# A graph convolution on one core: DVE kept free for the copies of x, strips 2 to 11 in two steps

## The chip, the cores and the metric

The kernel runs on one core of one Trainium2 chip. The metric is the device time of one execution in microseconds (us), as the median of several runs.

## The reference

```python
# x: (8192, 128), adj: (8192, 8192), w: (128, 128), all fp32
A = adj + jnp.eye(adj.shape[0], dtype=adj.dtype)
deg = jnp.sum(A, axis=1)
d_isqrt = jax.lax.rsqrt(deg)
A_hat = A * d_isqrt[:, None] * d_isqrt[None, :]
h = jnp.matmul(A_hat, x)
y = jax.nn.elu(jnp.matmul(h, w))
out = _layernorm(x + y, axis=-1)
```

The matrix adj has 256 MiB. A product with rows of x needs the row sums of adj for those rows first, since x is scaled by d_isqrt before it is multiplied.

## The kernel before

adj is cut into 16 x 16 tiles of 512 x 512 (1 MiB each). Tile (t, u) holds the rows of strip u and the columns of band t. Strip r is the 16 tiles (0..15, r); when all its row sums are known, x of band r can be scaled, and only then can any tile of column r be multiplied. PE multiplies a column's tiles two to four at a time (a "part", L1016, 64 matmuls of 128 to 512 columns, each of which stands as two records in the trace), so that 256 records belong to 4 tiles when each matmul is 256 wide. Parts of one job gather in one of two PSUM sets.

A tile (t, r) with t < r comes after x of band t is known: it is loaded once ("first"), summed by ACT (L916), turned by DVE (a transposition of 32 x 32 blocks, L1035), multiplied, and its product is added to hT by DVE (L1060, L1062). A tile (t, r) with t >= r has to be loaded for the row sums of strip r before x of band t exists. Some of these are kept in SBUF until then ("near": the table KEPT says how many diagonals back for each column, 56 in all); the others are only summed ("far", four staging slots) and loaded a second time at the end ("again", 80 tiles). SBUF has 23 slots of one tile; a load waits on the SP queue (L824 to L855) until the slot's tenant has been multiplied.

How x of a band comes to be ready, for each strip: ACT's last row sum of the strip; DVE adds the sums up (L1042, the row sum reduction); POOL takes the power -0.5 (L881), and scales x (L888); then 16 copies spread x over the four quadrants: pair (s, q) is the rows of quarter s for quadrant q. The pairs (0, q) are needed for the first matmuls of a part: (0, 0) and (0, 1) are copied by DVE (L1049), (0, 2) and (0, 3) by ACT (L924). POOL copies the other twelve (L899). POOL also adds the unit matrix to the diagonal tile (L874). For the strips in HALVED, 3 to 9, the whole chain is done in two steps, blocks 0 and 1 first and then blocks 2 and 3 ("half 0" and "half 1"): the strip's near loads come in two halves, and PE may multiply one or two parts by half 0 alone while half 1 is being made.

The order of all this is fixed before the kernel is built: the function plan() walks through a rough model of the engines and writes for each engine a list of operations, picking at each moment, among what is ready for an engine, the one of the lowest rank (x's copies, reductions and scalings 0, adds 1, transpositions 4 or 6). FEED is the number of tiles that should wait for PE before the plan turns from first tiles to the next strip's rows. Each engine then executes its list in order, with semaphores; the plan's times are not in the kernel, only its order.

Of the kernel before, what the change touches and what calls it, by code (L numbers as in the profile page):

```python
# [7 lines left out]
Q = 4  # L8
BAND = 512
BANDS = N // BAND  # L10
BLOCKS = BAND // 128
# [1 line left out]
SLOTS = 23  # L13
STAGE = 4
LATE = 3
KEPT = (1, 2, 3, 4, 5, 6, 5, 4, 5, 4, 3, 4, 3, 2, 3, 2)
AHEAD = 2
STAY = 10
WIDTHS = (4, 2)
XN = 1  # L20
HALVED = range(3, 10)
HALF_JOBS = 2
PIECES = 2
RING = 4
SETS = 2
MERGE = 4
FEED = 10
FLIGHT = 4
EPS = 1e-5
LAST = 2  # L30
FIRST_COPIES = [("dve", [(0, 0), (0, 1)]), ("act", [(0, 2), (0, 3)]), ("pool", [(s, q) for s in (1, 2, 3) for q in range(Q)])]
LATE_COPIES = [("act", [(s, q) for q in range(Q)]) for s in range(Q)]


# [40 lines left out]
def plan():  # L75
# [28 lines left out]
    firsts, queued, rest, backlog = [], [], [], 0  # L104
    held_diagonals = {}
    group_at, group_todo, group_open, group_job = -1, [], [], None
    pending_x = []

    def offer(engine, rank, kind, arg, took):
        nonlocal serial  # L110
# [13 lines left out]
    def allowed(kind, arg):  # L124
        if kind == "out":
            return free_set() is not None and counts["residuals"] > 0 and counts["w"] > 0 and (counts["outs"] == counts["z"] or not parts_left())
        if kind == "z":
            return counts["stored"] >= arg - RING + 1
        return True

    def parts_left():
# [2 lines left out]
    def release(slot):  # L134

        if rows_done and len(late) < LATE:
            tenants[slot].append(("late", len(late)))
            late.append(slot)
            if len(late) == LATE:
                offer("act", 0, "residuals", 0, 0.6)  # L140
        else:
            free.append((now, slot))
# [183 lines left out]
    def close_stage():  # L326

        nonlocal stage_open
        if stage_open and rows_done and not far_open:
            stage_open = False  # L330
            for slot in range(STAGE):
                tenants[slot].append(("stage", 0))
                release(slot)

    def row_summed(load):

# [219 lines left out]
    while True:  # L556
        issue()
        for e in ready:
            if until[e] <= now:
# [9 lines left out]
                elif e == "pe" and (arg := next_part()) is not None:  # L569
                    kind, long = "part", took(len(parts[arg][2])) * (1.0 if parts[arg][5] is None else 1 / PIECES) + (1.75 if now - until["pe"] > 2.5 else 0.0)  # L570
                    lone_before = len(parts[arg][2]) == 1
                else:
                    continue
                order[e].append((kind, arg))
                until[e] = now + long
                busy[e] += long
# [554 lines left out]
```

## Time and profile before

| | |
|---|---|
| median of 3 runs | 1052.9 us (1051.27 to 1054.26) |
| the profiled execution | 1054.86 us, of which the span is 1053.1 us |
| PE busy | 924.1 us (88%) |
| DVE busy | 772.1 us (73%) |
| ACT busy | 702.9 us (67%) |
| POOL busy | 213.1 us (20%) |
| bytes moved by DMA | 368.37 MB, mean 350 GB/s |
| mean granted clock of PE | 0.968 |

The span is the time from the first to the last instruction; the execution's own time is 1.8 us longer. Busy shares are means over stages with different limits: in the first 680 us the DMA engines are full, in the rest PE is.

### The profile page before, as it was taken

What the parts mean: (1) busy time and instruction counts of PE and PEld (TensorE: products, weight loads), DVE (VectorE), ACT (ScalarE), POOL (GpSimd) and SP (SyncE); (2) the same over time, 40 slices, a digit from 0 to 9 for tenths busy, and PEclk for the clock granted to TensorE, in tenths of its full rate; (3) what the DMA queues carried; (4) which work ended last, traced back from release to release, by engine and by line L of the source; (5) the groups of instructions that cost most, each with busy time, mean ns of one, the idle gap of its engine ahead of it and who ended that gap; (6) DMA issues with size and microseconds to landing.
All of it is one profiled execution on the core that took longest, in us unless ns stands there. A gap on an engine that the chain in (4) does not pass through costs nothing.

```text
span 1053.1 us, 36270 instructions
## 1 busy us (share of the span) xinstructions
PE 924.1 (88%) x16256; PEld 858.6 (82%) x16256; DVE 772.1 (73%) x649; ACT 702.9 (67%) x1667; POOL 213.1 (20%) x365
## 2 busy tenths in 40 slices
PE   0089399399797998999999999999999999999995
PEld 0066288399797997999899999899889999999994
DVE  0496497576776768686879787887999698866923
ACT  6898798889988898988888988862132518131201
POOL 0120120210502204050522533457011001000000
PEclk9999789799998998999999999999999999999998
DMA  9999999999999999999999999977999888999920
GB/s 384 401 394 407 399 393 400 396 395 395 384 399 356 377 392 397 388 396 396 394 397 395 384 392 392 338 247 262 386 385 341 292 280 293 307 298 315 348 76 21
DMA packets 168092, 368.37 MB, mean 350 GB/s; under 512 B 6528, under 2 KB 33280, under 8 KB 159232
## 3 DMA queue, kind: packets, MB, share of 16 engines
q1 hardware_dynamic: 150896, 357.59, 91.1%
q10 hardware_dynamic: 17040, 8.46, 2.7%
q8 instruction: 128, 2.10, 0.8%
q14 instruction: 28, 0.23, 0.1%
HBM read 361.82 MB, written 4.19 MB: 348 GB/s over the span
## 4 chain that ended last, share of the span: by engine, by line
PE 66%; DMA 11%; POOL 7%; DVE 6%; issue 6%; ACT 3%; SPq 1%; POOLq 0%; ACTq 0%; DVEq 0%
PE p_set L1016 65%; DMA space<-in_adj 8%; POOL space L899 5%; DVE space L1035 4%; DMA xn<-in_x 3%; ACT space L916 1%; PE p_set L994 1%; ACT space L924 1%; POOL xn L888 1%; SPq L855 1%; DVE hT L1060 1%; POOL d L881 1%; POOL space L874 0%; DVE space L1049 0%; DVE stats L1096 0%
## 5 line engine op out<-in xcount | busy, mean ns | idle before, releaser
L1016 PE MATMUL p_set<-space 32*128 32x256 f32 (+2 forms) x16128 | 907.6, 383 | 115.8 <-DVE space L1035 55.4
L1016 PEld LDWEIGHTS p_set<-space 32*128 32x128 f32 x16128 | 843.2, 188 | 176.0 <-issue 121.2
L1035 DVE STREAM_TRANSPOSE space<-space 128x2048 f32<-128x2048 f32 x256 | 580.2, 2293 | 96.8 <-ACT space L916 69.9
L916 ACT ACTIVATE space<-space 128x512 f32<-128x512 f32 (+3 forms) x732 | 576.8, 790 | 80.7 <-DMA space<-in_adj 76.1
L1060 DVE TENSOR_TENSOR hT<-p_set,hT 128x1024 f32<-128x1024 f32 (+1 forms) x104 | 106.8, 1040 | 125.0 <-PE p_set L1016 124.8
L899 POOL COPY space<-xn 32x256 f32<-32x256 f32 (+1 forms) x276 | 134.2, 486 | 18.1 <-POOL space L874 1.5
L916 ACT ACTIVATION_READ_ACCUMULATOR space<-space 128x1 f32 x732 | 137.5, 188 | 0.0
L881 POOL TENSOR_TENSOR d<-deg,minus_half 128x2 f32<-128x2 f32 (+1 forms) x23 | 19.0, 827 | 517.5 <-DVE deg L1042 517.2
L939 ACT ACTIVATE space<-space 128x512 f32<-128x512 f32 x16 | 10.1, 632 | 161.4 <-DVE space L1071 161.3
L924 ACT ACTIVATE space<-xn 32x512 f32<-32x512 f32 (+1 forms) x110 | 63.1, 573 | 76.8 <-POOL xn L888 73.3
L906 POOL TENSOR_TENSOR rstd<-var_eps,minus_half 128x4 f32<-128x4 f32 x16 | 16.9, 1056 | 231.7 <-DVE var_eps L1105 231.6
L947 ACT ACTIVATE space<-space,shift,rstd 128x128 f32<-128x128 f32 x60 | 24.7, 481 | 22.3 <-DVE shift L1111 22.3
L888 POOL TENSOR_TENSOR xn<-xn,d 128x256 f32<-128x256 f32 (+1 forms) x27 | 22.1, 820 | 67.1 <-DMA xn<-in_x 65.5
L1049 DVE COPY space<-xn 32x256 f32<-32x256 f32 (+1 forms) x46 | 26.5, 576 | 11.0 <-POOL xn L888 10.0
L994 PEld LDWEIGHTS p_set<-ident,hT 128*128 128x128 f32 x128 | 15.4, 191 | 6.7 <-issue 4.3
L874 POOL TENSOR_TENSOR space<-space,ident 128x512 f32<-128x512 f32 x16 | 20.4, 1276 | 0.7
L994 PE MATMUL p_set<-ident,hT 128*128 128x128 f32 x128 | 18.2, 287 | 1.7 <-DVE hT L1060 1.7
L1062 DVE COPY hT<-p_set 128x1024 f32<-128x1024 f32 (+2 forms) x6 | 9.5, 1580 | 13.9 <-PE p_set L1016 13.9
L1090 DVE SCALAR_TENSOR_TENSOR space<-space 128x512 f32<-128x512 f32 x16 | 10.6, 663 | 11.1 <-ACT space L941 10.9
L1096 DVE BATCH_NORM_STATS2 stats<-space 128x6 f32<-128x128 f32 x64 | 14.0, 282 | 0.5
L1042 DVE TENSOR_REDUCE deg<-sums 128x2 f32<-128x34 f32 (+1 forms) x23 | 4.1, 178 | 13.7 <-ACT space L916 13.7
L1071 DVE TENSOR_TENSOR space<-p_set,d 128x512 f32<-128x512 f32 x16 | 10.8, 673 | 2.9 <-PE p_set L994 2.8
(16 smaller groups left out, 38.2 us busy)
## 6 DMA issues: line engine op xcount, KB each, us to landing
space<-in_adj SPq DMA_DIRECT2D x309, 1024.0 KB, 13.5
space<-in_adj SPq DMA_DIRECT2D x30, 512.0 KB, 10.7
space<-in_adj SPq DMA_DIRECT2D x16, 768.0 KB, 13.9
xn<-in_x SPq DMA_DIRECT2D x20, 256.0 KB, 11.4
space<-in_x ACTq DMA_DIRECT2D x16, 256.0 KB, 7.4
out_rows<-space ACTq DMA_DIRECT2D x16, 256.0 KB, 9.3
ident<-in_w ACTq DMA_DIRECT2D x1, 64.0 KB, 6.2
```

The costliest lines, as they stand in the source:

```text
L874: nc.gpsimd.tensor_tensor(on_diagonal, on_diagonal, ident[:, :].unsqueeze(1).to_broadcast([128, BLOCKS, 128]), ALU.add)\
L881: nc.gpsimd.tensor_tensor(d[:, r, blocks], deg[:, r % 2, blocks], minus_half[:, blocks], ALU.pow).then_inc(d_ready, 1)
L888: nc.gpsimd.tensor_tensor(xn[:, h % XN, blocks], xn[:, h % XN, blocks], d[:, t, blocks].unsqueeze(2).to_broadcast([128, many, F]), ALU.mul ...
L899: nc.gpsimd.tensor_copy(xs_part(h, half, q, s), x_part(h, half, s)).then_inc(copied_by["pool"], 1)
L916: ins = nc.scalar.activation(view[:, g], view[:, g], ACT.Copy, accum_out=to[:, g:g + 1])
L924: nc.scalar.activation(xs_part(h, half, q, s), x_part(h, half, s), ACT.Copy).then_inc(copied_by["act"], 1)
L947: ins = nc.scalar.activation(pos[:, n % RING, b], pos[:, n % RING, b], ACT.Identity, bias=shift[:, n % RING, b:b + 1], scale=rstd[:, n % R ...
L994: ins = nc.tensor.matmul(p[:, 0, F * b:F * (b + 1)], hT[:, at:at + 128], w_sb[:, :], start=True, stop=True)
L1016: ins = nc.tensor.matmul(to, xs_chunk(h, j)[quadrant(q)], moving, start=first and s == 0 and b == blocks_of(half).start, stop=last and s = ...
L1035: nc.vector.transpose(slots[slot], slots[slot]).then_inc(tile_turned, 1)
L1049: nc.vector.tensor_copy(xs_part(h, half, q, s), x_part(h, half, s)).then_inc(copied_by["dve"], 1)
L1060: nc.vector.tensor_tensor(rows, new, rows, ALU.add).then_inc(product_added, 1)
```

## The change

Four tables and one rule of the plan change.

- FIRST_COPIES: all four pairs (0, q) are DVE's; ACT copies none for the first use of a band.
- HOLD = 8: for strips 0 to 7, from the moment the plan gives ACT the last row sum of a strip (or of a half), DVE gets no transposition that would take 2.4 and no add that would take 1.3 beyond the end of that sum, until it has got the copies of that x.
- HALVED: strips 2, 10 and 11 are now also done in two steps.
- FEED 14 in place of 10.
- KEPT: column 15 keeps four tiles in place of two, so that (15, 12) and (15, 13) are loaded once. Loads of adj go from 336 to 334 MiB.

```diff
--- before.py
+++ after.py
@@ -13,22 +13,23 @@
 SLOTS = 23
 STAGE = 4
 LATE = 3
-KEPT = (1, 2, 3, 4, 5, 6, 5, 4, 5, 4, 3, 4, 3, 2, 3, 2)
+KEPT = (1, 2, 3, 4, 5, 6, 5, 4, 5, 4, 3, 4, 3, 2, 3, 4)
 AHEAD = 2
 STAY = 10
 WIDTHS = (4, 2)
 XN = 1
-HALVED = range(3, 10)
+HALVED = range(2, 12)
 HALF_JOBS = 2
 PIECES = 2
 RING = 4
 SETS = 2
 MERGE = 4
-FEED = 10
+FEED = 14
 FLIGHT = 4
+HOLD = 8
 EPS = 1e-5
 LAST = 2
-FIRST_COPIES = [("dve", [(0, 0), (0, 1)]), ("act", [(0, 2), (0, 3)]), ("pool", [(s, q) for s in (1, 2, 3) for q in range(Q)])]
+FIRST_COPIES = [("dve", [(0, q) for q in range(Q)]), ("pool", [(s, q) for s in (1, 2, 3) for q in range(Q)])]
 LATE_COPIES = [("act", [(s, q) for q in range(Q)]) for s in range(Q)]
@@ -126,6 +127,8 @@
             return free_set() is not None and counts["residuals"] > 0 and counts["w"] > 0 and (counts["outs"] == counts["z"] or not parts_left())
         if kind == "z":
             return counts["stored"] >= arg - RING + 1
+        if kind in ("turn", "add") and urgent:
+            return now + (2.4 if kind == "turn" else 1.3) <= min(urgent.values())
         return True
@@ -331,6 +334,19 @@
+    def last_sum(load):
+
+        r = load[3] if load[0] == "tile" else load[1]
+        k0, nk = (0, BLOCKS) if load[0] == "tile" else load[2:4]
+        wide = 1 if load[0] == "tile" else load[5] if load[0] == "near" else load[5] // BAND
+        for half in halves_of(r):
+            many = BLOCKS if half is None else BLOCKS // PIECES
+            base = many * half if half is not None else 0
+            rows = len(set(range(k0, k0 + nk)) & set(range(base, base + many)))
+            if rows and sums_left[r, half] == rows * wide:
+                return r, half
+        return None
@@ -571,6 +587,10 @@
                     lone_before = len(parts[arg][2]) == 1
                 else:
                     continue
+                if kind == "sum" and (row := last_sum(loads[arg])) is not None and row[0] < HOLD:
+                    urgent[row] = now + long + 0.1
+                elif kind == "copies" and e == "dve" and (homes[arg[0]][0], arg[1]) in urgent:
+                    del urgent[homes[arg[0]][0], arg[1]]
                 order[e].append((kind, arg))
                 until[e] = now + long
                 busy[e] += long
```

What this does to the order of DVE, at strip 7. TENSOR_REDUCE is the row sum reduction of a half, COPY from xn are the copies of x, STREAM_TRANSPOSE a tile's transposition, TENSOR_TENSOR on hT an add. Before:

```order
L1060 TENSOR_TENSOR hT<-p_set,hT 128x4x8x32 x2
L1042 TENSOR_REDUCE deg<-sums 128x2
L1049 COPY space<-xn 32x2x128 x2
L1035 STREAM_TRANSPOSE space<-space 128x4x512
L1042 TENSOR_REDUCE deg<-sums 128x2
L1060 TENSOR_TENSOR hT<-p_set,hT 128x4x8x32
L1035 STREAM_TRANSPOSE space<-space 128x4x512
L1049 COPY space<-xn 32x2x128 x2
L1035 STREAM_TRANSPOSE space<-space 128x4x512 x2
```

And now, at the same place:

```order
L1080 TENSOR_TENSOR hT<-p_set,hT 128x4x4x32 x2
L1062 TENSOR_REDUCE deg<-sums 128x2
L1069 COPY space<-xn 32x2x128 x4
L1062 TENSOR_REDUCE deg<-sums 128x2
L1069 COPY space<-xn 32x2x128 x4
L1080 TENSOR_TENSOR hT<-p_set,hT 128x4x8x32
L1055 STREAM_TRANSPOSE space<-space 128x4x512
L1080 TENSOR_TENSOR hT<-p_set,hT 128x4x8x32
L1055 STREAM_TRANSPOSE space<-space 128x4x512 x3
```

Two adds stood directly ahead of the first reduction, and two transpositions and one add between it and the second copies; now one job's add (in two pieces) stands ahead of it, and nothing but the four copies and the second reduction behind it, until both halves have been copied.

POOL at strips 10 and 11. The first TENSOR_TENSOR on d is the power, the one on xn the scaling, the one on space the unit matrix added to the diagonal tile, COPY the twelve copies of x. Before:

```order
L881 TENSOR_TENSOR d<-deg,minus_half 128x4
L888 TENSOR_TENSOR xn<-xn,d 128x512
L874 TENSOR_TENSOR space<-space,ident 128x4x128
L899 COPY space<-xn 32x4x128 x12
L881 TENSOR_TENSOR d<-deg,minus_half 128x4
L888 TENSOR_TENSOR xn<-xn,d 128x512
L874 TENSOR_TENSOR space<-space,ident 128x4x128
L899 COPY space<-xn 32x4x128 x12
```

And now, for strip 10 (strip 11 is alike):

```order
L901 TENSOR_TENSOR d<-deg,minus_half 128x2
L908 TENSOR_TENSOR xn<-xn,d 128x256
L919 COPY space<-xn 32x2x128 x12
L901 TENSOR_TENSOR d<-deg,minus_half 128x2
L908 TENSOR_TENSOR xn<-xn,d 128x256
L919 COPY space<-xn 32x2x128 x12
L894 TENSOR_TENSOR space<-space,ident 128x4x128
```

The chain is done twice on half the elements, and the diagonal tile is now served behind all copies.

PE multiplies the same number of tiles before its first use of the x of each strip as before, for every strip; strips 10 and 11 come 8 tiles apart.

The SP queue loads the same amount before the last load of each strip's row sums, except for strips 2, 10 and 11, whose first half is complete after 72.0, 227.0 and 237.75 MiB, where the whole was at 74.5, 228.5 and 238.75.

## Rows read from the trace of the kernel before

**Rows 1.** The page: its span, busy time of each engine, and two of the lines of 40 slices.

```profile
span 1053.1 us, 36270 instructions
...
PE 924.1 (88%) x16256; PEld 858.6 (82%) x16256; DVE 772.1 (73%) x649; ACT 702.9 (67%) x1667; POOL 213.1 (20%) x365
...
PE   0089399399797998999999999999999999999995
...
DMA  9999999999999999999999999977999888999920
```

**Rows 2.** Timeline of PE: start, duration, instructions, and in brackets the idle time before.

```profile
55.39 58.24 PE L1016 MATMUL p_set<-space 32*128 32x256 f32 x768 [55.39 <-DVE space L1035]
134.15 58.35 PE L1016 MATMUL p_set<-space 32*128 32x256 f32 x1024 [20.52 <-ACT space L924]
209.56 58.12 PE L1016 MATMUL p_set<-space 32*128 32x256 f32 x1024 [17.05 <-ACT space L924]
272.19 8.66 PE L1016 MATMUL p_set<-space 32*128 32x256 f32 x112 [4.51 <-DVE space L1049]
...
336.71 9.35 PE L1016 MATMUL p_set<-space 32*128 32x256 f32 x128 [5.67 <-ACT space L924]
...
400.22 110.16 PE L1016 MATMUL p_set<-space 32*128 32x256 f32 x1984 [4.48 <-DVE space L1049]
511.89 2.93 PE L1016 MATMUL p_set<-space 32*128 32x256 f32 x48 [1.51 <-ACT space L924]
515.53 115.11 PE L1016 MATMUL p_set<-space 32*128 32x256 f32 x2128 [0.70 <-POOL space L899]
...
633.49 26.18 PE L1016 MATMUL p_set<-space 32*128 32x256 f32 x480 [0.69 <-POOL space L899]
...
662.60 71.08 PE L1016 MATMUL p_set<-space 32*128 32x256 f32 x1312 [0.69 <-POOL space L899]
734.49 14.10 PE L1016 MATMUL p_set<-space 32*128 32x256 f32 x256 [0.82 <-issue]
```

**Rows 3.** Timeline of all engines, 499 to 518 us, where x of strip 7 is made.

```profile
500.06 0.19 ACT L916 ACTIVATION_READ_ACCUMULATOR space<-space 128x1 f32 x1
500.09 1.23 DVE L1060 TENSOR_TENSOR hT<-p_set,hT 128x1024 f32<-128x1024 f32 x1 [4.81 <-PE p_set L1016]
...
501.23 0.18 DVE L1042 TENSOR_REDUCE deg<-sums 128x2 f32<-128x34 f32 x1
...
502.95 5.55 POOL L899 COPY space<-xn 32x256 f32<-32x256 f32 x12
...
508.58 0.70 POOL L881 TENSOR_TENSOR d<-deg,minus_half 128x2 f32<-128x2 f32 x1
...
509.36 0.61 POOL L888 TENSOR_TENSOR xn<-xn,d 128x256 f32<-128x256 f32 x1
...
510.04 5.44 POOL L899 COPY space<-xn 32x256 f32<-32x256 f32 x12
...
510.36 0.67 DVE L1049 COPY space<-xn 32x256 f32<-32x256 f32 x2
...
510.94 0.85 ACT L924 ACTIVATE space<-xn 32x256 f32<-32x256 f32 x2
```

**Rows 4.** Windows of 10 us: busy us of each engine, granted clock, DMA share, GB/s.

```profile
310.00:320.00 10.00, 10.00 (x192) 9.50 (x188) 8.35 (x5) 9.19 (x25) 0.00 (x0) 1.00 1.03 402
320.00:330.00 10.00, 10.00 (x193) 9.49 (x189) 4.15 (x3) 8.12 (x17) 0.00 (x0) 1.00 0.81 294
350.00:360.00 10.00, 10.00 (x192) 10.00 (x191) 6.88 (x4) 7.16 (x13) 0.00 (x0) 1.00 0.95 337
```

**Rows 5.** Waits of the SP queue, 312 to 326 us: total, times, longest.

```profile
SPq L824 <- PE p_set L1016: 6.5, 1, 6.5
```

**Rows 6.** Groups by line and shape: the copies of x by half a strip.

```profile
L1049 DVE COPY space<-xn 32x256 f32<-32x256 f32 x28 | 10.8, 386 | 3.5 <-POOL xn L888 3.0
```

**Rows 7.** Window 440 to 480 us, where PE never waits.

```profile
440.00:480.00 40.00, 40.00 (x748) 39.07 (x745) 31.59 (x23) 35.23 (x83) 13.51 (x29) 1.00 1.04 392
```

More of the change, by code:

```diff
@@ L106, in plan @@
     group_at, group_todo, group_open, group_job = -1, [], [], None
-    pending_x = []
+    pending_x, urgent = [], {}
     def offer(engine, rank, kind, arg, took):
```

## The prediction

> **What bounds the kernel now.** I read the page first [rows 1]: PE is busy for 924.1 of 1053.1 us, and its slices are low at the start and around slices 5 to 13; the DMA engines are full until slice 26. So an early stretch is paced by loads and a later one by PE. Next the timeline of PE [rows 2]. It starts at 55.39 and then stops at the head of nearly every strip: 20.52 us before strip 1, 17.05 before strip 2, 4.51, 5.67 and 4.48 before strips 3, 4 and 5, and 1.51 inside strip 7. Each stop is named after a copy of x, by ACT or DVE. From 515.53 to the end there is no stop above 1 us except small ones between the last jobs.
>
> Such stops don't add up. A stop ends when the x of its strip is ready, and that is set by the strip's last load and sum, not by how far PE was. What PE gains at strip 1 it waits out at strip 2. The end is set by the last stop, here the second half of strip 7 at 511.89, and by what PE loses behind it. That is the main thing to see: of 54 us of stops, only the last one and what follows it are for sale.
>
> **The change part by part.** The sum is made against the profiled execution, 1054.86 us, of which 1053.1 is the span; the median of the runs, 1052.9, lies 2.0 below it.
>
> *Term A, the chain of strip 7* [rows 3]. ACT's last sum for the first half ends at 500.06 + 0.19 = 500.25. The reduction is issued at 501.23, because an add (500.09, 1.23 us) stands in front of it. The new order has one job's add there, older by a part, and holds back others from the start of the last sum; so the reduction can go at 500.28, 0.95 earlier. Power and scaling follow, then POOL's twelve copies, 5.55 us. The second half's power, 508.58, starts the moment these end, so it moves by 0.95 too, to 507.63, and the scaling from 509.36 to 508.41, ending 509.02. DVE then makes four copies. One costs between 0.67/2 = 0.34 [rows 3] and, if each waits its turn beside POOL, POOL's own pace of 5.44/12 = 0.45; the mean of all is 0.386 [rows 6]. I take 0.45, since here all four lie beside POOL's: 1.8, to 510.9. PE starts at 511.0 where it was 511.89, and POOL's last copy, on which it waits at 515.53, is 0.95 earlier. A = 0.9, between 0.5 and 1.3. What ACT's copies cost before is the same size: 510.94 + 0.85.
>
> One rule of the Trainium skill speaks against this. In the rows, DVE's two copies (510.36 to 511.03) lie inside POOL's twelve, which took 5.44 us, and at 502.95 they took 5.55: POOL's pace is 0.11 apart at most. The page "SBUF — State Buffer", section "Who interferes with whom", says that a DVE copy of this kind takes the port pair that it shares with GpSimd for the whole instruction, and the other blocks. By that rule two more DVE copies of 0.34 would push POOL's twelve by 0.7 in each half, 1.4 over the two, and A would be -0.5. The trace agrees that DVE pays, and shows little of POOL paying. The case is among the rivals.
>
> *Term B, loads no longer stopped by PE* [rows 4, 5]. The DMA share is 1.03 at 310 to 320, falls to 0.81 in the next 10 us and is 0.95 at 350 to 360. In 312 to 326 the SP queue waited 6.5 us for PE to give a slot back. So (1.03 - 0.81) x 10 = 2.2 us and (1.03 - 0.95) x 10 = 0.8 us of full-rate loading were lost, 3.0 in all, and everything loaded behind it came later, strip 7's rows too. PE leaves strips 3 and 4 earlier: strip 3's and strip 4's first copies were both late behind DVE's transpositions and ACT's sums, which the new order takes away, some 1 to 2.5 us each (a transposition of 2.3 us stood ahead of the copies). Then slots come free that much sooner. B is between 0 (the plan's new order blocks at another slot) and 3.0; I take 2.0, since the first dip is cut by about 1 and the second vanishes.
>
> *Term C, strips 10 and 11 in two steps* [rows 2]. PE's full pace is 115.11/2128 = 54.1 ns a record. From 633.49 to 662.60, from the last wait of strip 10 to that of strip 11, it executed one strip's 8 tiles, 512 records, which need 27.7 us; it took 29.11. The loss of 1.4 is PE's first part running ahead of POOL's twelve whole copies, 0.69 of it shown as a wait and the rest as stretched matmuls. Strip 10 has the same wait, so 2.8 for both. With two steps PE first takes half a part while POOL makes the other half's copies. Strip 10's first half is loaded 1.5 MiB ahead of the whole; a MiB takes 1.05 MB / 392 GB/s = 2.7 us [rows 7], so 4 us earlier, which is enough. Strip 11's is 1 MiB ahead, 2.7 us, less than POOL's 5.44 for a half, so its second half may be late. C is 0 to 2.8; I take 2.5.
>
> *Term D, column 15* [rows 2]. PE idles 0.82 us at 734.49 for a transposed tile of column 15, one of the two that are loaded again. These are now in SBUF since their strip. D = 0.8, bounds 0 and 0.8. The two loads saved are worth nothing more: the page's DMA digits fall under 9 from slice 26 on.
>
> *Costed at nothing.* Strip 2 in two steps, and the earlier starts of strips 1 to 5: they shorten stops that later stops absorb. FEED: it moves first tiles ahead of far rows, within the same amount of loads. The single (5, 15) part: it costs a few tenths before strip 7's stop. The diagonal behind the copies: its tile isn't in a first part. The cover of all of these is the stop at strip 7. Strip 7's stop itself gets longer to look at, since PE arrives earlier: its half part can't end before POOL's twelfth copy, 508.50 - 0.95 = 507.55, and a quarter of the part behind it (16 records, 0.9), so at 508.4; the stop is then up to 2.6 us.
>
> What the hold costs: during it DVE's queue stands. In 440 to 480 DVE is busy 31.59 of 40 us [rows 7]; over a strip of 16 tiles, 1024 records or 55.4 us, that is 43.8, and with 8 x 0.45 less the 4 x 0.386 it did already, 45.9. So 9.5 us are free. Held per half: up to 2.4 ahead of the sum's end, and 0.2 + 0.7 + 0.6 and two gaps, 1.7, behind it; 8.2 for both. It fits, by 1.3 us at worst.
>
> Sum: 0.9 + 2.0 + 2.5 + 0.8 = 6.2. 1054.86 - 6.2 = 1048.7 for a profiled execution, 1046.7 for the median; I say 1047.
>
> **The rivals.** A measurement of this kernel tells 0.3%, 3.2 us, from no change.
>
> *The gain stays under 3.2 us.* B is 0 because the loads block elsewhere, and either C fails at strip 11 or the longer stop at strip 7 lets PE's clock fall. At 4.48 us of idle the restart took 110.16 for 1984 records, 107.3 at full pace: 2.8 lost. At 1.51 us nothing of the kind shows. A stop of 2 to 3 us lies between. 0.9 + 2.5 + 0.8 - 2.8 = 1.4, so 1051.5. For it: 2 to 3 us is not far from 4.5. Against it: the shortest such stop that cost a clock drop is 4.48. Chance 0.2.
>
> *The copies hold each other up.* POOL's copies of both halves at strip 7 are stretched by the two added DVE copies of 0.34, 1.4 in all. 6.2 - 1.4 = 4.8 faster, so 1048. For it: where DVE's copy came first, POOL's twelve took 5.55 instead of 5.44. Against it: that is 0.11, not 0.7. Chance 0.1.
>
> *DVE becomes the bound, and the kernel is slower.* Place: strips 3 to 7, the transpositions after a hold. It decides once what is held per strip passes the 9.5 us that are free, which adds that wait on PE for parts would bring about. Price: one transposition, 2.3 us, late in each of five strips, 11.5; less A, C and D, 4.2; 7.3 slower, 1060. For it: DVE also idles in its queue behind adds that wait for PE, so its free time isn't free at will. Against: before strip 7's stop this would have to be more than the stop absorbs. Chance 0.1.
>
> *More than 10 us faster.* The plan's order changes the last 300 us as well, and the outputs' waits there; and loads gain the full 3.0. A + 3.0 + 2.8 + 0.8 and 3 us in the last stage, 10.5: 1042. Chance 0.1.
>
> *The change doesn't do what it says.* Strips 8 to 11 aren't held; there a transposition can still stand ahead of four copies. Then second halves are ready up to 2.3 late, and C is eaten: 1049.5. This lies in my range and is faster.
>
> **How the numbers follow.** Likeliest, A to D in about this size: 0.5, with a range of its own of 1044 to 1050. Copies hold each other up: 0.1. Under 3.2: 0.2. Slower: 0.1. Much faster: 0.1. The range of 1042 to 1054.5 leaves out most of the slower case and half of the much faster one, under 2 in 10. Faster by over 0.3%: 0.5 + 0.1 + 0.1 = 0.7, of which I take off 0.02 for a likeliest case that ends short, 0.68. Within 0.3%: 0.22. Slower: 0.1.
>
> **What would show it.** In the timeline of PE: stops at strips 2 to 5, and at strip 7 a stop of 2 to 3 us that ends at 508 to 511 rather than 511.89; full pace from there; no stretch at strips 10 and 11; no wait for column 15. DMA share 1.0 in the windows where it was 0.81. In DVE's timeline four copies right behind each scaling. Wrong if: PE waits on L1055 transpositions in strips 3 to 9, or if strip 8 or 9 has a new stop, or if the stops at strips 3 to 5 still end within 0.5 us of where they ended.

## The result, and the profile after

The changed kernel takes 1046.9 us (median of 6 runs, 1046.31 to 1047.35); the kernel before, measured beside it, 1053.22 (6 runs, 1051.27 to 1054.26). The ratio is 0.994, 95% interval 0.993 to 0.995: 6.3 us faster. On another chip the changed kernel took 1047.0 again, the kernel before 1055.15, which is 8.2 us (ratio 0.9925, 0.9909 to 0.9940): the gain lies between 6 and 8 us. The prediction was 1047.0, range 1042 to 1054.5.

The page of the changed kernel, its span and busy times, which answer to [rows 1]:

```profile
span 1045.5 us, 35982 instructions
...
PE 922.2 (88%) x16128; PEld 847.3 (81%) x16128; DVE 791.2 (76%) x723; ACT 684.1 (65%) x1613; POOL 222.8 (21%) x407
```

DVE is busy for 19 us more, ACT for 19 less: the copies have changed engine, and there are more of them. The timeline of PE, which answers to [rows 2]:

```profile
198.75 5.62 PE L1036 MATMUL p_set<-space 32*128 32x256 f32 x64 [7.29 <-DVE space L1069]
...
270.31 5.68 PE L1036 MATMUL p_set<-space 32*128 32x256 f32 x64 [8.09 <-DVE space L1069]
...
335.02 11.75 PE L1036 MATMUL p_set<-space 32*128 32x256 f32 x176 [4.31 <-DVE space L1069]
...
395.28 17.51 PE L1036 MATMUL p_set<-space 32*128 32x384 f32 x256 [1.74 <-DVE space L1069]
...
508.48 87.85 PE L1036 MATMUL p_set<-space 32*128 32x256 f32 x1584 [2.04 <-DVE space L1069]
596.87 146.19 PE L1036 MATMUL p_set<-space 32*128 32x256 f32 x2704 [0.54 <-POOL space L919]
742.98 1.16 PE L1014 MATMUL p_set<-ident,hT 128*128 128x128 f32 x8
```

PE restarts with strip 7's second half at 508.48 where it was 511.89. The stop ahead of it is 2.04 us, not 1.51, because PE now comes to it earlier. Behind it there is one small stop, 0.54 in strip 9, until the first output at 742.98; the waits of strips 10 and 11 and of column 15 are gone. The chain of strip 7, which answers to [rows 3] (timeline of all engines):

```profile
497.78 0.18 ACT L936 ACTIVATION_READ_ACCUMULATOR space<-space 128x1 f32 x1
...
497.99 0.19 DVE L1062 TENSOR_REDUCE deg<-sums 128x2 f32<-128x34 f32 x1 [1.36 <-ACT space L936]
...
499.72 5.52 POOL L919 COPY space<-xn 32x256 f32<-32x256 f32 x12
...
502.43 0.19 DVE L1062 TENSOR_REDUCE deg<-sums 128x2 f32<-128x34 f32 x1 [1.14 <-ACT space L936]
...
505.32 0.69 POOL L901 TENSOR_TENSOR d<-deg,minus_half 128x2 f32<-128x2 f32 x1
...
506.74 1.59 DVE L1069 COPY space<-xn 32x256 f32<-32x256 f32 x4 [4.12 <-POOL xn L908]
```

The reduction is issued 0.03 us after the last sum (497.78 + 0.18 = 497.96), where it had stood 0.98 behind an add. The second half's reduction is done at 502.62, but its power runs only at 505.32, when POOL has ended its twelve copies: 2.7 us of waiting for POOL that no order of these copies on DVE can shorten. Windows (busy us of PE, its weight load, DVE, ACT, POOL, then clock, DMA share, GB/s), answering to [rows 4], and one later stretch:

```profile
320.00:330.00 10.00, 10.00 (x192) 9.50 (x188) 3.83 (x3) 8.70 (x19) 0.00 (x0) 1.00 0.85 306
350.00:360.00 10.00, 10.00 (x192) 9.50 (x188) 9.99 (x6) 8.24 (x18) 0.00 (x0) 1.00 1.04 387
520.00:560.00 40.00, 40.00 (x748) 38.40 (x744) 38.47 (x32) 33.36 (x77) 13.62 (x29) 1.00 1.04 399
```

The second dip of the DMA share has vanished (0.95 to 1.04), the first is hardly smaller (0.81 to 0.85). And DVE, which was busy 31.07 of 40 us at 520 to 560 in the kernel before, is now busy 38.47 there. Read as work that the holds kept back, this is likely, but no run separates it.

Where the 7.5 us between the two profiled executions came from, by three points of PE's timeline: 3.4 us by strip 7's restart (511.89 to 508.48), 5.5 by the first output (748.52 to 742.98), and 7.5 by the end (1054.86 to 1047.35). The profiled execution of before was 1.6 us above its median and that of the changed kernel 0.4 above, so in the medians it is 6.3.

### The profile page after: what moved, and what is told of

The parts are those of the page before. It is cut to its first block, busy times and chain, and to the rows that moved or that the text cites. A ratio compares the mean times of both kernels' runs of the same rounds, so it can differ in the third digit from the quotient of the medians.

```text
span 1045.5 us, 35982 instructions
## 1 busy us (share of the span) xinstructions
PE 922.2 (88%) x16128; PEld 847.3 (81%) x16128; DVE 791.2 (76%) x723; ACT 684.1 (65%) x1613; POOL 222.8 (21%) x407
## 4 chain that ended last, share of the span: by engine, by line
PE 62%; issue 13%; DMA 13%; POOL 6%; ACT 3%; DVE 2%; SPq 1%; POOLq 0%; ACTq 0%; DVEq 0%
PE p_set L1036 61%; DMA space<-in_adj 9%; POOL space L919 4%; DMA xn<-in_x 3%; ACT space L936 2%; PE p_set L1014 2%; DVE space L1055 1%; SPq L875 1%; POOL xn L908 1%; POOL d L901 1%; DVE space L1069 1%; POOL space L894 0%; DVE hT L1080 0%; ACT space L967 0%; DVE stats L1116 0%
## 5 line engine op out<-in xcount | busy, mean ns | idle before, releaser
L1036 PE MATMUL p_set<-space 32*128 32x256 f32 (+3 forms) x16000 | 905.9, 383 | 110.5 <-DVE space L1055 76.5
L1036 PEld LDWEIGHTS p_set<-space 32*128 32x128 f32 x16000 | 831.9, 187 | 180.1 <-issue 117.4
L936 ACT ACTIVATE space<-space 128x512 f32<-128x512 f32 (+2 forms) x728 | 576.5, 793 | 108.3 <-DMA space<-in_adj 99.2
L1080 DVE TENSOR_TENSOR hT<-p_set,hT 128x512 f32<-128x512 f32 (+1 forms) x116 | 106.7, 940 | 68.5 <-PE p_set L1036 68.1
L919 POOL COPY space<-xn 32x256 f32<-32x256 f32 (+1 forms) x312 | 142.4, 456 | 19.7 <-POOL space L894 0.7
L1069 DVE COPY space<-xn 32x256 f32<-32x256 f32 (+1 forms) x104 | 47.5, 457 | 37.7 <-POOL xn L908 35.3
L944 ACT ACTIVATE space<-xn 32x512 f32<-32x512 f32 x64 | 40.1, 627 | 46.1 <-POOL xn L908 43.6
L1082 DVE COPY hT<-p_set 128x1024 f32<-128x1024 f32 (+3 forms) x7 | 9.5, 1364 | 11.0 <-PE p_set L1036 11.0
```

Of the source, the lines that this page charges most:

```text
L919: nc.gpsimd.tensor_copy(xs_part(h, half, q, s), x_part(h, half, s)).then_inc(copied_by["pool"], 1)
L936: ins = nc.scalar.activation(view[:, g], view[:, g], ACT.Copy, accum_out=to[:, g:g + 1])
L944: nc.scalar.activation(xs_part(h, half, q, s), x_part(h, half, s), ACT.Copy).then_inc(copied_by["act"], 1)
L1036: ins = nc.tensor.matmul(to, xs_chunk(h, j)[quadrant(q)], moving, start=first and s == 0 and b == blocks_of(half).start, stop=last and s = ...
L1069: nc.vector.tensor_copy(xs_part(h, half, q, s), x_part(h, half, s)).then_inc(copied_by["dve"], 1)
L1080: nc.vector.tensor_tensor(rows, new, rows, ALU.add).then_inc(product_added, 1)
```

## The experiments

All times are medians. Three groups ran on three chips; on them the kernel before took 1054.47, 1055.15 and 1054.80 us. Two kinds are to be kept apart. Where a table is changed, plan() writes another order of loads as well; where DVE's work is lengthened or its list is altered behind the plan, everything else stands as it was. The second kind is the cleaner.

### The hold, undone in the table, and strips 10 and 11 whole again

```diff
-HOLD = 8
+HOLD = 0
```

*HOLD 0.* 

> The changed kernel with HOLD = 0: DVE isn't kept free, all else as changed. Theory 1: x of strips 3 to 7 is ready 1 to 3 us later, the last stop ends at 509.5 to 511, and the loss is 1 to 2.5 us: 1048 to 1049.5. Theory 3, that strips 10 and 11 and column 15 give the whole gain and the hold nothing: 1046.9 within 0.7.

Measured: 1055.87, ratio 1.001 (1.000 to 1.002). The whole gain is gone, but not in the way that was expected. The load order differs from about its 30th entry on. PE's timeline and one window of this kernel:

```profile
318.37 20.62 PE L1036 MATMUL p_set<-space 32*128 32x256 f32 x384 [4.30 <-issue]
343.88 57.69 PE L1036 MATMUL p_set<-space 32*128 32x256 f32 x1024 [4.89 <-DVE space L1069]
...
320.00:330.00 10.00, 10.00 (x151) 9.41 (x148) 7.05 (x4) 6.57 (x22) 0.00 (x0) 0.78 0.19 62
```

The DMA share falls to 0.19 in one window, PE waits 4.30 us for a tile, and strip 4 restarts 8.9 us later than in the changed kernel. That lateness is much the same at the end, 8.5 us in the profiled executions. So this run says what a bad load order costs, and not what the hold is worth.

```diff
-HALVED = range(2, 12)
+HALVED = range(2, 10)
```

*Strips 10 and 11 whole.* 

> The changed kernel with HALVED up to 9 only, so that strips 10 and 11 are whole again. Term C: PE loses 1.4 us at each of strips 10 and 11, 2.5 to 3 us slower, 1049.5 to 1050. If C was worth nothing: 1046.9.

Measured: 1068.44, ratio 1.013 (1.012 to 1.015). The timeline of PE:

```profile
627.27 34.82 PE L1036 MATMUL p_set<-space 32*128 32x256 f32 x640 [1.80 <-DVE space L1069]
...
734.10 26.25 PE L1036 MATMUL p_set<-space 32*128 32x256 f32 x436 [16.16 <-DVE space L1069]
```

The expected loss at strip 10 is there, 1.80 us. But a stop of 16.16 us at strip 14 comes with it. The waits of the SP queue, 680 to 720 us (total, times, longest), say why:

```profile
SPq L875 <- PE p_set L1036: 17.4, 1, 17.4
SPq L844 <- PE p_set L1036: 14.8, 1, 14.8
```

For 32.2 us it waited for PE to give slots back: this plan put rows of strip 14 into slots whose tiles PE hadn't multiplied. A second experiment in which the plan, not the edit, sets the time.

So the third undoing took a value at which only two of the loads move:

```diff
-HALVED = range(2, 12)
+HALVED = range(2, 11)
```

*Strip 11 alone whole.* 

> The changed kernel with strip 11 whole again; all loads but two stand where they stood. Theory 1 (term C, 1.4 us for each of strips 10 and 11): 1.2 to 1.5 us above the changed kernel, 1048.3, and a stretched stretch or a stop at strip 11 alone. Theory 2 (strip 11's half comes too late to help, its loads are only 2.7 us apart and POOL takes 5.5): within 0.4 us of the changed kernel.

Measured: 1049.32 (1047.95 to 1050.18), ratio 0.9949 (0.9937 to 0.9961), against 1046.9 and 1047.0 of the changed kernel on other chips: 2.3 us above it. The trace has the one new wait that was expected, for strip 11's copies:

```profile
652.91 5.46 PE L1036 MATMUL p_set<-space 32*128 32x256 f32 x96 [0.79 <-DVE space L1069]
```

but its profiled execution, at 1047.95 the shortest of the five, reaches the first output at 743.49, only 0.5 after the changed kernel. Counting PE's records behind the restart, at 508.48 in both, says more. The 2624th, just ahead of strip 11's wait, starts 143.3 us behind it here and 144.4 in the changed kernel, so this kernel was 1.1 ahead by then; from there to the first output it takes 91.7 us for 90.1. Strip 11 in one step costs 1.6 in these traces, against term C's 1.4. The lead came from two things: there is no stop at strip 9, and the clock did not fall behind a stop as long as the changed kernel's (timeline of PE, and the window, which answer to those of the changed kernel further down):

```profile
508.48 3.19 PE L1036 MATMUL p_set<-space 32*128 32x256 f32 x48 [2.05 <-DVE space L1069]
...
510.00:520.00 10.00, 9.27 (x168) 8.07 (x164) 8.22 (x5) 9.24 (x30) 3.28 (x7) 1.00 1.05 390
```

### A delay put ahead of DVE's copies, all orders kept

```diff
                     wait_vacant(dve, ("home", h))
+                    if homes[h][0] == 4:
+                        nc.vector.tensor_reduce(idle[:, half:half + 1], minus_half[:, 0:1].unsqueeze(2).to_broadcast([128, 1, 3000]), AX.X, ALU.add)
                     for s, q in copies_of(h)[some][1]:
```

*Strip 4.* 

> The changed kernel, with 3.2 us of idle work on DVE (a reduction of 3000 elements of a constant) put ahead of the copies of x of each half of strip 4; order of everything else untouched. Theory 1, that only the last stop (strip 7) sets the end: PE restarts 3 us later at strip 4, the stops at strips 5 to 7 absorb it, total within 1 us of the changed kernel, 1046.9 (ratio to before 0.994). Theory 2, that stops add up: 3 to 6 us slower, 1050 to 1053.

*Strip 7 (the same with == 7).* 

> The same idle work at strip 7 instead. Theory 1: the second half's x is ready 3.2 us later, the stop at 508.5 becomes 511.7, and nothing behind it can absorb it: 3.2 us slower, 1050.1 (ratio 0.997). A fall of PE's clock in the longer stop would add up to 2.8. Theory 2, stops add up: the same as at strip 4.

Measured: 1048.8 (ratio 0.9950, 0.9938 to 0.9962) with the delay at strip 4, and 1047.89 (0.9952, 0.9936 to 0.9967) at strip 7. The reduction took 3.28 us. Timeline of PE, the delay at strip 4 first, then that at strip 7:

```profile
338.07 8.65 PE L1037 MATMUL p_set<-space 32*128 32x256 f32 x128 [7.31 <-DVE space L1072]
...
397.88 17.51 PE L1037 MATMUL p_set<-space 32*128 32x384 f32 x256 [0.95 <-DVE space L1072]
...
510.87 29.38 PE L1037 MATMUL p_set<-space 32*128 32x256 f32 x508 [2.04 <-DVE space L1072]
```

```profile
511.97 28.30 PE L1037 MATMUL p_set<-space 32*128 32x256 f32 x468 [3.32 <-DVE space L1072]
```

The rule "only the last stop counts" fails here. 3.05 us at strip 4 are 2.6 at strip 5 and still 2.4 at strip 7, where the stop itself is unchanged, 2.04: both the arrival of PE and the last sum have moved. ACT's last sum of strip 7's first half ends at 500.36 with the delay at strip 4, and at 497.96 without. Against the run with the delay at strip 7, which is the changed kernel up to there and ran on the same chip, strips 4 and 5 restart 2.9 and 2.3 later (335.13 and 395.54 there); another execution of the unaltered kernel, the control below, has them 0.9 and 0.75 us later than that by itself, so differences under 1 us between two traces mean little. The loads show the way that the lateness took. At 350 to 360, where the changed kernel had a DMA share of 1.04, it is:

```profile
350.00:360.00 10.00, 10.00 (x192) 10.00 (x191) 10.00 (x7) 6.86 (x14) 0.00 (x0) 1.00 0.87 303
```

Of the 2.4 at strip 7, 1.45 are left at the first output (744.43 for 742.98): the changed kernel's stop of 0.54 at strip 9 is gone and took part of the delay.

At strip 7 itself the delay moved the restart by 3.5 us and gave two levels of time: four runs at 1047.6 to 1047.9 and two at 1051.5 and 1052.1, the profiled execution among the latter. The slower level is what the first theory said with a fall of the clock (1050.1 and up to 2.8), the faster one is 1 us above the changed kernel and fits no theory. The only trace is one of the slower, so this stays open.

*Strips 3 to 7, each half, 2.5 us (the same with 3 <= homes[h][0] <= 7, and 2250 elements).* 

> All orders and loads as in the changed kernel, but DVE does an idle reduction of about 2.35 us ahead of its copies of x of each half of strips 3 to 7: the place where the kernel before had a transposition. Theory 1 (only the last stop sets the end): strip 7 alone counts. Its first half comes 2.35 later, POOL's copies aren't delayed by it, the second half's copies come 2.35 later: strip 7 restarts at 510.8, and the time is 1049.2. Theory 2 (PE's lateness comes back as later slots and later loads, term B read backwards): strips 3 to 6 add to it; in a run with 3 us more at strip 4 alone strip 7 restarted 2.4 later, so here strip 7 restarts at 512 to 513 and the DMA share near 320 us falls below 0.85: the time is 1050.5 to 1052. Theory 3 (hold is worth nothing, C and D are all): within 1 us of the control.

The control beside it, the changed kernel unaltered: 

> The changed kernel again, unaltered, beside three variants of it whose load order is its own. All theories: 1046.9 within 1 us, ratio to the kernel before 0.993 to 0.995; strip 7's first part starts near 508.5 us, with a stop of 2 us ahead of it.

Measured: control 1047.0 (1046.37 to 1048.46), ratio 0.9925 (0.9909 to 0.9940). With the delays 1055.05 (11 runs), ratio 0.9999 (0.9989 to 1.0010): 8 us more than the control. All theories had it too low. PE's timeline with the delays:

```profile
272.98 6.35 PE L1037 MATMUL p_set<-space 32*128 32x256 f32 x64 [10.73 <-DVE space L1072]
...
341.73 58.29 PE L1037 MATMUL p_set<-space 32*128 32x256 f32 x1024 [6.78 <-DVE space L1072]
403.60 62.52 PE L1037 MATMUL p_set<-space 32*128 32x384 f32 x1088 [3.58 <-DVE space L1072]
...
517.50 233.24 PE L1037 MATMUL p_set<-space 32*128 32x256 f32 x4288 [3.23 <-DVE space L1072]
...
280.00:290.00 10.00, 8.82 (x132) 8.80 (x136) 8.82 (x7) 8.45 (x20) 3.27 (x6) 0.83 0.69 243
320.00:330.00 10.00, 10.00 (x193) 10.00 (x189) 6.86 (x4) 9.44 (x23) 0.00 (x0) 1.00 0.76 270
```

In the control strips 3, 4, 5 and 7 restart at 271.21, 336.03, 396.29 and 509.44. The lateness grows: 1.8, 5.7, 7.3 and 8.1 us. Behind the dips of the DMA share (0.69, 0.76 and, at 350 to 360, 0.95, where the control has 0.95, 0.82 and 1.04) the last sum of strip 4's first half ends 3.3 later than in the control, strip 5's 4.7, strip 7's 4.65. That is term B with its sign turned: PE late, slots late, loads late, the next strip's sums late. The other 3.4 at strip 7 are the delay of its second half, 2.5, and an add that has come to stand ahead of the first half's reduction, 0.9.

That the time equals the kernel before is chance. Strip 7 restarts at 517.50, 5.6 us later than the 511.89 of before: ten delays of 2.5 us are more than the hold had removed. From there to the end of the execution it takes 537.6 us, where the kernel before took 543.0. So behind strip 7 the changed order is worth 5.4 us here, and 4.1 in the changed kernel itself, where the stop at strip 9 takes part of it.

### The copies alone put first, in the order of before

```diff
+    first_use = {h for h, (t, _) in enumerate(homes) if all(v != t for v, _ in homes[:h])}
...
+    for op in [op for op in order["dve"] if op[0] == "copies" and 3 <= homes[op[1][0]][0] <= 7]:
+        order["dve"].remove(op)
+        order["dve"].insert(order["dve"].index(("row_sum", (homes[op[1][0]][0], op[1][1]))) + 1, op)
```

> The kernel before with its loads and plan unchanged; only DVE makes all four copies (0, q), and for strips 3 to 7 they stand directly behind the strip's own reduction, so that no transposition or add comes between (adds ahead of the reduction stay). Theory 1 (terms A and B of the prediction, without the rest): strips 3 and 5 restart 2 to 2.5 us earlier, strip 4 1 us; the last sums of strip 7 come 1 to 2.3 earlier, and strip 7 itself by that; the time is 1.5 to 3 us under the kernel before. Theory 2 (the hold is the whole gain, as the idle reductions at strips 3 to 7 suggest, which took all of it away): 5 to 7 us under it, 1047 to 1049. Theory 3 (strips 10 and 11 and column 15 are the gain): within 1 us of the kernel before.

Measured: 1062.25 (1060.05 to 1066.76), ratio 1.007 (1.006 to 1.009): 7.5 us slower, against every theory, mine included. The profiled execution was the slowest of the six, 1066.76. DVE's timeline of this kernel at strip 4, then its PE:

```profile
338.22 1.60 DVE L1056 COPY space<-xn 32x256 f32<-32x256 f32 x4 [1.51 <-POOL xn L895]
339.85 6.70 DVE L1042 STREAM_TRANSPOSE space<-space 128x2048 f32<-128x2048 f32 x3
346.48 0.14 DVE L1049 TENSOR_REDUCE deg<-sums 128x2 f32<-128x34 f32 x1
```

```profile
339.97 8.72 PE L1023 MATMUL p_set<-space 32*128 32x256 f32 x128 [4.63 <-DVE space L1056]
...
420.24 45.18 PE L1023 MATMUL p_set<-space 32*128 32x256 f32 x832 [1.45 <-DVE hT L1067]
```

The copies now follow the reduction by 1.5 us, POOL's power and scaling, and DVE idles for it. But what was moved behind them, three transpositions of 6.70, stands in front of the second half's reduction: its sum ended at 344.46 and it was issued at 346.47. There are new waits for hT in PE's timeline, 1.45 us in strip 5 and 1.64 in strip 6, so DVE's adds are late too; but the changed kernel has such a wait of 1.74 at 414.52 and is fast with it. 5.2 us of the loss stand at strip 7's restart (517.05 for 511.89). So copying first isn't the gain by itself. The rule of the change also clears the time ahead of a reduction and keeps the second half free, and the plan finds other places for the transpositions. The hold on its own was never measured: here the rest of the rule is missing, and with HOLD 0 the loads changed.

### Strips 10, 11 and column 15 alone

```diff
-KEPT = (1, 2, 3, 4, 5, 6, 5, 4, 5, 4, 3, 4, 3, 2, 3, 2)
+KEPT = (1, 2, 3, 4, 5, 6, 5, 4, 5, 4, 3, 4, 3, 2, 3, 4)
...
-HALVED = range(3, 10)
+HALVED = range(3, 12)
```

> The kernel before with only strips 10 and 11 in two steps and column 15's two more tiles kept; its plan is the same load for load up to strip 9. Theory 1 (terms C and D of the prediction): strip 7 restarts at 511.9 as before, no stretched matmuls at strips 10 and 11, no wait for column 15, 3.3 us faster: ratio 0.997. Theory 2 (hold is everything): within 0.5 us of the kernel before. Theory 3 (from strip 7's restart to the end the changed kernel is 4 us shorter than before, which is C, D and a last stage of its own): 4 us faster, ratio 0.996. A plan of its own behind strip 9 can also bring a new stop there, which the timeline would show.

The edit is made to the kernel before. Measured: 1053.77 (12 runs), ratio 0.9995 (0.9982 to 1.0009): no change. Yet the terms are there. PE's timeline:

```profile
511.86 233.34 PE L1016 MATMUL p_set<-space 32*128 32x256 f32 x4288 [2.72 <-ACT space L924]
745.13 1.16 PE L994 MATMUL p_set<-ident,hT 128*128 128x128 f32 x8
749.95 8.88 PE L1016 MATMUL p_set<-space 32*128 32x256 f32 x128 [3.66 <-DVE hT L1060]
```

From the same restart as before, 511.86, PE runs without a stop to the first output at 745.13, where it was 748.52: 3.4 us, where 2.5 + 0.8 was predicted. Behind its stop of 2.72 the clock fell, to a mean of 0.83 at 510 to 520, and by the 368th record behind the restart PE had lost 0.6 to the kernel before; the two terms themselves brought 4.0. Then it waits 3.66 us for one add of DVE and takes 8.88 us for 128 records that take 7.19 elsewhere; the granted clock at 750 to 760 is 0.83. DVE at that place, and PE in the kernel before:

```profile
744.30 4.48 DVE L1035 STREAM_TRANSPOSE space<-space 128x2048 f32<-128x2048 f32 x2
...
748.71 1.19 DVE L1060 TENSOR_TENSOR hT<-p_set,hT 128x1024 f32<-128x1024 f32 x1
```

```profile
750.98 7.19 PE L1016 MATMUL p_set<-space 32*128 32x256 f32 x128 [1.30 <-DVE hT L1060]
```

DVE has two transpositions in front of the add that PE needs; in the kernel before there were three, and the add came at 749.73. Whatever PE gains before 750 us in this order, it gives back there. The changed kernel has no such wait.

### Who copies, and how many

*ACT copies (0, 2) and (0, 3) again, in the changed kernel's order.*

```diff
+MADE_COPIES = [("dve", [(0, 0), (0, 1)]), ("act", [(0, 2), (0, 3)]), ("pool", [(s, q) for s in (1, 2, 3) for q in range(Q)])]
...
-        return FIRST_COPIES if first_home(h) else LATE_COPIES
+        return MADE_COPIES if first_home(h) else LATE_COPIES
```

> All orders and loads as in the changed kernel, but pairs (0, 2) and (0, 3) of x are copied by ACT as before, put into its order where DVE's copies start. Theory 1 (who copies hardly matters): DVE's two take 0.8 us, ACT's two 0.85 beside them, but behind a sum of up to 1.9; the first use of a half is 0.7 earlier to 1.2 later, so the time is within 1.2 us of the control. Theory 2 (each DVE copy holds POOL up for its whole length): POOL's twelve copies shrink from 5.53 to 4.8 us in each half, strip 7's second half is ready 0.7 to 1.4 earlier, and the time falls by as much. Theory 3 (ACT is the late one, as the stops of the kernel before that are named after it suggest): strips 3 to 7 are late by 1 to 2 us each behind ACT's sums, and the time is 2 us or more above the control.

Measured: 1048.09 (1047.77 to 1049.16), 1.1 above the control, with intervals that overlap (0.9922 to 0.9951, and 0.9909 to 0.9940): the first theory, and the second is refuted. POOL's twelve copies at strip 7 take 5.55 us beside two copies of DVE and 5.55 in the control beside four. PE's stops at strips 3, 4, 5 and 7 are now all named after ACT, as those of before were, yet little hangs on them.

*DVE copies eight pairs, POOL eight.*

```diff
+MADE_COPIES = [("dve", [(s, q) for s in (0, 1) for q in range(Q)]), ("pool", [(s, q) for s in (2, 3) for q in range(Q)])]
```

> All orders and loads as in the changed kernel, but DVE also copies the four pairs (1, q), behind its first four, and POOL only eight. Theory 1 (POOL's twelve copies bound the second halves of strips 7 and 9): at strip 7 the second half's sum was ready 2.7 us before POOL had ended the first half's copies; eight take 3.7 instead of 5.53, so the second half is ready 1.8 earlier and PE restarts near 506.7 with a stop under 0.5; at strip 9 the 1.2 us of lateness goes. The time is 2 to 3 us under the control. Theory 2 (each DVE copy holds POOL up for its whole length of 0.34): POOL's eight copies still take 3.7 + 4 x 0.34 = 5.1, the gain is at most 0.5 us. Theory 3 (DVE is short of time): 16 more copies of 0.4 a strip delay the transpositions; new stops at strips 3 to 5 or inside them, and the time is above the control.

Measured: 1064.03, ratio 1.009 (1.007 to 1.010), 17 us above the control. Strip 7's chain, timeline of all engines:

```profile
500.08 3.44 DVE L1070 COPY space<-xn 32x256 f32<-32x256 f32 x8 [1.51 <-POOL xn L909]
500.11 3.72 POOL L920 COPY space<-xn 32x256 f32<-32x256 f32 x8
...
503.91 0.70 POOL L902 TENSOR_TENSOR d<-deg,minus_half 128x2 f32<-128x2 f32 x1
```

POOL's eight copies take 3.72, 0.465 each, as the twelve did with 5.55 / 12 = 0.463. The first theory was right so far: from the first scaling's end to the second power it is 3.8 us instead of 5.6. All of it reached PE: the second half's first 16 records start at 507.07, behind a stop of 0.39 and 2.4 before the control's 509.44; 0.5 of that is an earlier last sum. That is what the first theory had said. Then the third theory took over (all waits of PE, 520 to 750 us):

```profile
PE p_set L1037 <- DVE hT L1081: 8.4, 4, 3.1
```

The control has no wait in that stretch. This is the rival "DVE becomes the bound", and its place is behind strip 8.

*The same for strips 0 to 7 only.*

```diff
-        return FIRST_COPIES if first_home(h) else LATE_COPIES
+        return LATE_COPIES if not first_home(h) else MADE_COPIES if homes[h][0] < HOLD else FIRST_COPIES
```

> All orders and loads as in the changed kernel; DVE makes eight copies and POOL eight for strips 0 to 7 only, and as in the changed kernel from strip 8 on, where DVE is busy 39 of 40 us and with eight copies came to stop PE. Theory 1 (the loss with eight copies everywhere was all behind strip 8): strip 7 restarts 0.6 us earlier than the control, no stop behind it; 1046.4, within 1 us of the changed kernel. Theory 2 (a loss stays in strips 3 to 7, whose transpositions come later): more than 1 us above the changed kernel, with waits for hT or for tiles inside strips 3 to 6.

Measured: 1046.45 (1046.02 to 1047.02), ratio 0.9924 (0.9911 to 0.9937). PE at strip 7:

```profile
506.71 1.15 PE L1037 MATMUL p_set<-space 32*128 32x256 f32 x16 [0.28 <-DVE space L1070]
508.46 2.87 PE L1037 MATMUL p_set<-space 32*128 32x256 f32 x48 [0.60 <-DVE space L1070]
```

The second half begins at 506.71, 1.8 before the changed kernel, and no stop there is above 0.65. The first output comes at 741.64, 2.5 before the control and 1.3 before the profile after. That is the lowest median of all, but 0.5 us under the changed kernel on another chip is within what the runs scatter. The window of 510 to 520 us in the kernel before, the changed kernel and the control:

```profile
510.00:520.00 10.00, 7.79 (x140) 6.62 (x136) 8.76 (x7) 9.93 (x33) 6.03 (x13) 1.00 1.05 396
510.00:520.00 10.00, 10.00 (x162) 8.93 (x158) 7.83 (x5) 9.40 (x30) 3.26 (x7) 0.84 1.05 389
510.00:520.00 10.00, 10.00 (x140) 9.31 (x136) 6.50 (x5) 9.52 (x30) 4.12 (x9) 0.72 1.05 389
```

Behind the stop of 2.04 and 2.05 us the granted clock fell, to a mean of 0.84 and 0.72 between the levels of 2.4 and 1.2 GHz. Behind 1.51 before and 0.60 here it stayed at 1.00, and so it did behind 2.05 with strip 11 whole and behind 2.04 with strips 10 and 11 whole. What the fall costs can be counted. PE's 368th record behind the restart starts 20.8 us after it in the kernel before, 21.1 in the two kernels with whole strips, 21.5 in the changed kernel and 22.8 in the control: 0.4 us in one execution, 1.7 in another. At the first output the control is only 0.2 further behind its restart than the changed kernel (234.7 and 234.5); it has no stop at strip 9.

## Why the prediction was right, by its steps

**The bound and the end.** Read rightly in its first half: the time follows the restart of strip 7. "What PE gains at strip 1 it waits out at strip 2. The end is set by the last stop" is too strong. Strip 2 began 10.8 us earlier (198.75 for 209.56) and strip 3 only 1.9 (270.31 for 272.19), which agrees; but a delay of 3.05 at strip 4 was not absorbed by strip 5, and 2.4 of it stood at strip 7. The prediction had the mechanism, as term B, and used it in one place only. In the changed kernel the last stop is at strip 9, and it takes up part of what happens at strip 7.

**A, 0.9.** Measured 1.1: strip 7 restarts 3.4 earlier, of which 2.3 are the last sum (500.25 to 497.96). The add ahead of the reduction was worth 0.95 as said. The four copies took 1.59, 0.40 each, against 0.45 taken. The second half still waits for POOL.

**The clock at strip 7.** Costed at nothing, and kept as a rival at 2.8. It came, smaller: 0.4 us in the profiled execution. The mean of 0.84 over 10 us is 1.6 us of PE's pace, but the wait of 0.70 for POOL behind the restart [rows 2] is gone with it, and more. The argument that failed is that the shortest stop with a clock drop is 4.48: at 2.04 to 2.05 there was one in three executions and none in two.

**B, 2.0.** Measured 2.3 by strip 7's last sum. Its rows bear less than that: of the two dips the second vanished as said, 0.9, the first shrank by 0.4 and not 1, a third at 280 to 290 grew by 0.4 (a share of 1.01 before, 0.97 now), and the queue's wait of 6.5 us [rows 5] is still 6.5. That lateness of PE comes back through the loads is shown by the delays; of the 2.3 the three windows explain 0.9, and the rest isn't traced. That the size came out is partly luck.

**C, 2.5, and D, 0.8.** By the edit alone 3.4 at the first output, and 4.0 without what the clock took behind its stop of 2.72; strip 11 alone 1.6. The terms were there and rather larger than said. From strip 7's restart to the first output it is 236.6 us in the kernel before, 233.3 with C and D alone, and 234.5 in the changed kernel (742.98 - 508.48). So 2.1 arrived, and 1.2 are missing. By PE's records they are lost between the 1072nd and the 2100th behind the restart: strip 9, whose x waits for POOL, with a new stop of 0.54 and matmuls stretched ahead of it. The prediction had named a new stop at strip 8 or 9 as a sign of error, and costed strip 9 at nothing.

**What it left out.** 2.0 us in the last 300 (7.5 less 5.5). The waits of 1.30, 0.26 and 0.25 us for DVE's adds behind the first output are gone, 1.8 of the 2.0. The prediction put them into a rival and into no term. So 6.2 was met by 1.1 + 2.3 + 2.1 + 2.0 = 7.5 in the profiled pair, 6.3 in the medians: the sum is right, and partly by errors that cancel.

**What it took for additive.** A to D were priced as separate goods. They aren't. With C and D alone nothing is gained (0.9995), although their 3.4 us are there until 745; and the copies put first in the old order lose 7.5. What is shown: DVE's lateness ahead of the copies of x costs time and adds up over the strips, and C and D need a DVE that isn't late at 745. Not shown is that the hold gives the latter. With idle work in all the hold's places PE still ran from the first output to the end in the changed kernel's time, so the changed plan's order behind strip 8 is the likelier cause; which of the tables made it was not separated.

**The copies hold each other up.** Refuted for POOL. By the groups of lines a POOL copy of half a strip takes 398 ns on average with two DVE copies beside twelve in the kernel before, 405 with two and 404 with four in the order of the changed kernel (ACT copying again, and the control), and 410 with eight beside eight. Two more DVE copies cost POOL nothing like 0.7 per half. The Trainium skill's page "SBUF — State Buffer", section "Who interferes with whom", has the engine that issues second fully blocked for the whole of the other's instruction where a DVE copy runs in a mode that takes the shared ports, which it says copies can enter. No run here shows the mode of these copies. POOL's eight in 3.72 us beside 3.44 of DVE don't agree with such blocking of POOL. DVE's own, 386 and 326 ns each with two, 378 with four and 408 with eight, don't settle it for DVE's side.

**DVE becomes the bound.** Rightly kept as a rival, and placed too early. The 9.5 us of free time were read from the kernel before, where 520 to 560 looks no fuller than 440 to 480 (31.07 and 31.59 of 40). In the changed kernel DVE is busy 38.47 of 40 there, behind the strips where the prediction looked for the trouble. With eight copies it stopped PE in that stretch and after it.

## What to carry to other kernels

Where loads wait for slots that the slow engine must free, a stop isn't absorbed by the next: follow one delay through two strips before calling the others free. Price an engine's spare time in the stretch where the work that an edit moves will land, not only in the one that it leaves. When two kernels restart at different times, count the instructions from the restart on before reading a loss off the clock. And where a planner writes the order, change its list behind the plan and keep the loads, or the experiment measures another plan; two of the three tables undone moved the time by more than the whole gain.

## Not expected of the hardware

A stop of PE of 2.04 to 2.05 us was sometimes enough for its granted clock to fall, and its length alone doesn't decide it. In the 10 us from 510 to 520 the mean was 0.84, 0.72 and 0.83 in three executions (changed kernel, control, delay at strip 4) and 1.00 in two (strip 11 whole, strips 10 and 11 whole), though PE did the same ahead of it in all five: a stop of 0.5 to 0.6, 16 records in 1.15 us, then the stop of 2.04 or 2.05. Behind 2.72 and 3.38 (C and D alone, ACT copying again) it was 0.83; behind 1.51 it stayed at 1.00. With two stops of 2.52 and 3.32 us, in the kernel with the delay at strip 7, it was 0.66:

```profile
510.00:520.00 10.00, 8.03 (x96) 7.47 (x100) 6.64 (x9) 9.55 (x32) 3.55 (x7) 0.66 1.05 390
```

That run's two levels of time, 4 us apart, may come from this; the mean granted clocks, 0.973 to 0.975 in the four shorter runs and 0.970 and 0.972 in the two longer, are too close to decide it, and of the shorter ones there is no profile, so it stays open. And POOL's copies keep their pace within 3%, 398 to 410 ns each, whether DVE makes two copies beside POOL's twelve or eight beside its eight.
